# Graph layer and two-of-eight experts: four finer edge groups sorted beside the gathers, expert choices beside the last sums, tiles of 128 tokens, results added into the output

## What is computed

```python
edge_index = jnp.stack([src, dst])
x = x + gnn(_layernorm(x), W1, b1, W2, b2, edge_index)   # agg = segment_sum(x[dst], src); mean = agg / max(cnt, 1)
                                                         # x @ W1.T + b1 + mean @ W2.T + b2
x = x + ffn(_layernorm(x), ...)                          # top 2 of 8 gate scores, softmax over the two
                                                         # y_e = relu(x @ w1[e].T + b1[e]) @ w2[e].T + b2[e]
```

## Time and profile before

| | us |
|---|---|
| median of 3 runs (3217.92 to 3227.65) | 3221.21 |
| span of the profiled execution, first to last instruction | 3186.2 |
| first gather of an edge chunk starts | 376.2 |
| last sum into `agg` starts | 2027.6 |
| expert stage (transposes of its first tile, to its last bias) | 2195 to 3106 |

### The profile page before, as it was taken

How to read it: one execution, slowest core, us unless ns; L and a number is a source line. 1 busy time by engine, 2 the same in 40 slices (tenths; PEclk the granted TensorE clock), 3 DMA queues, 4 the chain that set the end, 5 groups by cost and what they waited for, 6 DMA issues and landing times. The chain is left out here.

```text
span 3186.2 us, 48030 instructions
## 1 busy us (share of the span) xinstructions
PE 2074.3 (65%) x8300; PEld 1438.4 (45%) x8300; DVE 1359.1 (43%) x4519; ACT 1351.9 (42%) x4253; POOL 1193.9 (37%) x1295
## 2 busy tenths in 40 slices
PE   0078766665646655566555555657899888898980
PEld 0056523333323333333333333444777777777770
DVE  7988677555558555555223223464000000000005
ACT  5156634655644555565444444445222222222220
POOL 1011276444447544445666666100222222222220
PEclk9999856778765777777666666556999999999995
DMA  3001122212332222224322224520212221221217
GB/s 101 0 24 35 50 79 80 63 59 63 58 61 79 68 66 64 66 65 72 94 86 89 89 86 86 77 93 14 74 48 89 89 68 52 87 89 46 73 30 244
DMA packets 104790, 227.36 MB, mean 71 GB/s; under 512 B 23170, under 2 KB 63530, under 8 KB 100644
## 3 DMA queue, kind: packets, MB, share of 16 engines
q0 software_dynamic: 55296, 151.07, 18.1%
q1 hardware_dynamic: 49444, 75.77, 7.2%
HBM read 282.12 MB, written 33.93 MB: 99 GB/s over the span
## 5 line engine op out<-in xcount | busy, mean ns | idle before, releaser
L411 POOL DMA_INDIRECT arena<-ytab,stage x928 | 907.2, 978 | 346.5 <-issue 264.1
L694 PE MATMUL bank<-arena,onehot 128*128 128x257 f32 x1856 | 786.8, 535 | 334.2 <-issue 102.6
L694 PEld LDWEIGHTS bank<-arena,onehot 128*128 128x128 f32 x1856 | 425.1, 263 | 590.0 <-issue 352.8
L647 PE MATMUL bank<-ohc,val 125*128 125x336 f16 (+3 forms) x1796 | 412.0, 344 | 402.8 <-ACT val L486 210.1
L977 DVE TENSOR_TENSOR agg<-agg,bank 128x257 f32 x928 | 388.7, 419 | 596.0 <-PE bank L694 235.9
L486 ACT ACTIVATE val<-ohq,arena 125x128 f16<-125x128 f16 (+1 forms) x1370 | 462.9, 391 | 380.2 <-DVE ohq L883 282.6
L591 ACT ACTIVATE arena<-bank,agg 128x256 f32<-128x256 f32 x448 | 212.5, 474 | 683.4 <-PE bank L745 646.9
L647 PEld LDWEIGHTS bank<-ohc,val 125*128 125x128 f16 (+1 forms) x1796 | 155.6, 109 | 645.8 <-ACT val L486 317.6
L529 ACT ACTIVATE onehot<-away 128x128 f32<-128x128 f32 x928 | 277.7, 299 | 397.5 <-PE bank L694 185.7
L757 PE MATMUL bank<-agg,arena 128*128 128x256 f32 x1792 | 400.6, 382 | 0.0
L745 PE MATMUL bank<-xnT,agg 128*128 128x256 f32 x1792 | 398.8, 381 | 0.8 <-DVE xnT L1110 0.8
(11 more groups left out here) (148 smaller groups left out, 1173.1 us busy)
## 6 DMA issues: line engine op xcount, KB each, us to landing
agg<-in_w SPq DMA_DIRECT2D x112, 1024.0 KB
arena<-ytab,stage POOLq DMA_INDIRECT x928
agg<-ztab SPq DMA_DIRECT2D x12, 896.0 KB, 7.3
agg<-in_b SPq DMA_DIRECT2D x56, 128.0 KB
ytab<-yout SPq DMA_DIRECT2D x7, 896.0 KB, 4.1
xtab<-xn SPq DMA_DIRECT2D x49, 128.0 KB, 1.7
node<-in_x SPq DMA_DIRECT2D x4, 1536.0 KB
out<-node SPq DMA_DIRECT2D x6, 896.0 KB
```

The source lines that it names most:

```text
L411: pool.indirect_dma_start(out=rows[:, r, 0:D], out_offset=None, in_=ytab[:, :], in_offset=bass.IndirectOffsetOnAxis(ap=stage[:, r:r + 1], ...
L647: mm = pe.matmul(bank[4 + v][:, 0:n], val[0:lanes, u % RING[g], v, :], ohc[0:lanes, u % RING[g], 0:n], start=False, stop=False, skip_group ...
L694: pe.matmul(bank[r % NPS][:, 0:W], onehot[:, r % NPS, :], rows[:, r, :], start=True, stop=True).then_inc(s_agg, 1)
```

## The change

Most of the file is new; the arithmetic on features is as before, except where noted.

- **Edges.** Four groups (128, 176, 240, 256 columns). The edges of a group are sorted without padding to chunks and cut into *units* of 256 (two gathers): 63, 86, 118 and 125 units, 784 gathers. A *segment* is a unit's share of one source block: 589 run. Each takes two accumulating 257-column matmuls and one sum into `agg`. POOL's indices come straight from `rowidx`.
- **Ranks** come from PE: triangular f16 matmuls (`rank_part`) over one-hot tiles of 16 columns x 50 (`block_onehots`, 125x800 f16), picked out by DVE (`picked_ranks`).
- **Placing** goes by tiles of 8 columns, one DVE instruction for eight one-hots (`place_tile`); ACT scales 8 columns one at a time (4 of 8 in group 0).
- **Lane one-hots** of four segments are one DVE instruction (`lane_onehots`, 128x1024 f16), widened to float32 by one ACT instruction.
- **Order.** Everything about the segments is written out, no loop; `share(window, total, k)` spreads the sort of the next group over the segments k of this one. The W1 half of the linear layer moves from the start to beside the last group (`self_part`). The mean is taken out of the weights and not of x, so that x is transposed as it is.
- **Between the layers.** `tail(r)` does row r of h, moments, transposes, gates, choices and token sort beside the last 51 segments; blocks are done in the order in which the last units reach them. The first 14 blocks' tokens fill 10 early tiles from a table of their own (`xtab_a`), and the rest of the choices are made beside those tiles.
- **Experts.** T = 128, 106 tiles, `fetch` three tiles ahead. The softmax weight of each row is gathered too (`fetch_weights`, 4 bytes a row) and applied by DVE. h goes to `out` before, and `deliver` adds into `out` with an accumulating scatter that waits until the one before has landed. The end stage is gone.

The core of the diff:

```diff
-COLS = [229, 278, 293]
+COLS = [128, 176, 240, 256]
...
+HALVES = 2
+UNIT = HALVES * P
+UNITS = [-(-EP * c // UNIT) for c in COLS]
...
+SEGS = [-(-(u + NT - 1) // 8) * 8 for u in UNITS]
...
+RU = 8
+BACK = 4
+WIDE = 16
...
+PC = 8
...
+QUAD = 4
...
+NA = 10
...
+T = 128
...
-R = 16
...
-T = 256
```

Gathers, POOL. `s_free` counts units whose segments are multiplied:

```diff
-                        pool.indirect_dma_start(out=rows[:, r, 0:D], out_offset=None, in_=ytab[:, :],
-                                                in_offset=bass.IndirectOffsetOnAxis(ap=stage[:, r:r + 1], axis=0)).then_inc(s_row[r], 16)
...
-                    gathers(i, False)
+                pool.wait_ge(s_rowtab, g + 1)
+                for k in range(UNITS[g]):
+                    v = UNIT0[g] + k
+                    if v >= RU:
+                        pool.wait_ge(s_free, v - RU + 1)
+                    for h in range(HALVES):
+                        c = HALVES * k + h
+                        pool.indirect_dma_start(out=rows[:, v % RU, h, 0:D], out_offset=None, in_=ytab[:, :],
+                                                in_offset=bass.IndirectOffsetOnAxis(ap=rowidx[g % 2][:, c:c + 1], axis=0)).then_inc(s_row[v % RU], 16)
```

Segments, PE (new), and DVE:

```diff
+                        upto = [n_units & COUNTS for n_units in loaded(ENG.PE, need[g % 2], k // 2, m // 2, UNIT0[NG])]
+                    if k % QUAD == 0:
+                        pe.wait_ge(s_oh, n // QUAD + 1)
+                    if k % 2 == 0:
+                        pe.wait_ge(s_units, upto[k % 16 // 2])
+                    if n >= NPS:
+                        pe.wait_ge(s_sum, free_after(n))
+                    pair = rows_flat[:, bass.ds(at[k % 16], HALVES * W)]
+                    for h in range(HALVES):
+                        mm = pe.matmul(bank[bank_of(n)][:, 0:W], onehot[n // QUAD % 2][:, n % QUAD, h, :], pair[:, h * W:(h + 1) * W],
+                                       start=(h == 0), stop=(h == HALVES - 1))
+                    mm.then_inc(s_agg, 1)
+                    if k >= LAG:
+                        beside(g, k - LAG)
+                for k in range(RUN[g] - LAG, RUN[g]):
+                    beside(g, k)
...
+                    if k % 16 == 0:
+                        at = loaded(ENG.DVE, offs[g % 2], k, min(16, SEGS[g] - k), (NT - 1) * W)
+                    if k % QUAD == 0 and n // QUAD + 1 < SEG0[NG] // QUAD:
+                        lane_onehots(n // QUAD + 1)
+                    v.wait_ge(s_agg, n + 1)
+                    if n > 0:
+                        v.wait_ge(s_sum, n)
+                    a = agg[:, bass.ds(at[k % 16], W)]
+                    v.tensor_tensor(a, a, bank[bank_of(n)][:, 0:W], ALU.add).then_inc(s_sum, 1)
+                    beside(g, k)
```

Ranks picked, columns placed and lanes, DVE (new):

```diff
+                v.wait_ge(s_ta, k)
+                if t == 0:
+                    v.tensor_copy(c3[s % 2][0:NT, :], rank_a[0:NT, TH:TH + 3]).then_inc(s_c3, 1)
+                v.tensor_tensor(prod[0:EP, 0:TH], rank_a[0:EP, 0:TH], oh[j % OHB][0:EP, 0:TH], ALU.mult).then_inc(s_ma, 1)
+                v.wait_ge(s_tb, k)
+                v.tensor_tensor(prod[0:EP, TH:2 * TH], rank_b[0:EP, 0:TH], oh[j % OHB][0:EP, TH:2 * TH], ALU.mult).then_inc(s_mb, 1)
+                v.wait_ge(s_ma, k)
+                v.wait_ge(s_mb, k)
+                v.tensor_reduce(pos[0:EP, t * WIDE:(t + 1) * WIDE], prod[0:EP, :].rearrange("p (u b) -> p u b", b=BW), AX.X, ALU.add).then_inc(s_v, 1)
+                n_v.up()
...
+            def place_tile(s, i):
+
+                j, c = PT0[s] + i, i * PC
+                if j >= 2:
+                    v.wait_ge(s_pt, j - 1)
+                v.tensor_tensor(in_pairs(ohq[j % 2][0:EP]), counted(PC, P), pairs(pos_cq[0:EP, 1, c:c + PC, :], PC, P), ALU.is_equal).then_inc(s_q, 1)
+                v.tensor_tensor(in_pairs(ohc[j % 2][0:EP, :, 0:CH[s]]), counted(PC, CH[s]), pairs(pos_cq[0:EP, 0, c:c + PC, :], PC, CH[s]),
+                                ALU.is_equal).then_inc(s_c, 1)
+                v.wait_ge(s_q, j + 1)
+                if s == 0:
+                    m = PC - BY_ACT
+                    v.tensor_tensor(in_pairs(val[j % 2][0:EP, BY_ACT:PC, 0, :]), in_pairs(ohq[j % 2][0:EP, BY_ACT:PC]),
+                                    pairs(val1_2[0:EP, c + BY_ACT:c + PC, :], m, P), ALU.mult)
+                c += COL0[s]
+                v.tensor_tensor(in_pairs(val[j % 2][0:EP, :, 1, :]), in_pairs(ohq[j % 2][0:EP]), pairs(val2_2[0:EP, c:c + PC, :], PC, P), ALU.mult).then_inc(s_vd, 1)
...
+                    v.wait_ge(s_oh, q - 1)
+                m = QUAD * HALVES
+                v.tensor_tensor(onehot16[q % 2].rearrange("p k (m r) -> p k m r", r=2),
+                                lanes16[:, :].rearrange("p (a m r) -> p a m r", a=1, r=2).to_broadcast([P, m, P // 2, 2]),
+                                lane2[g % 2][:, k:k + QUAD].rearrange("p k h (a r) -> p (k h) a r", a=1).to_broadcast([P, m, P // 2, 2]),
```

Experts, POOL and DVE:

```diff
-            def deliver(j, b):
+            def fetch_weights(j, b):
+                table = ptab_a if isinstance(j, int) and j < NA else ptab
+                pool.wait_ge(s_pst, j + 1)
+                pool.sem_inc(s_pass)
+                for n in range(TT):
+                    pool.indirect_dma_start(out=weight[:, b, n:n + 1], out_offset=None, in_=table[:, :],
+                                            in_offset=bass.IndirectOffsetOnAxis(ap=pstage[:, b, n:n + 1], axis=0)).then_inc(s_pg[b], 16)
+
+            def deliver(j, b, landed):
                 pool.wait_ge(s_sst, j + 1)
                 pool.wait_ge(s_fo, j + 1)
+                if landed is not None:
+                    pool.wait_ge(s_sc2[1 - b], 16 * TT * landed)
                 pool.sem_inc(s_pass)
                 for n in range(TT):
-                    pool.indirect_dma_start(out=ztab[:, :], out_offset=bass.IndirectOffsetOnAxis(ap=sstage[:, b, n:n + 1], axis=0),
-                                            in_=ysb[:, b, n, :], in_offset=None).then_inc(s_sc2[b], 16)
+                    pool.indirect_dma_start(out=out[:, :], out_offset=bass.IndirectOffsetOnAxis(ap=sstage[:, b, n:n + 1], axis=0),
+                                            in_=ysb[:, b, n, :], in_offset=None, bounds_check=N - 1, oob_is_err=False,
+                                            compute_op=ALU.add).then_inc(s_sc2[b], 16)
...
                     v.wait_ge(s_sc2[b], half * 16 * TT)
-                v.tensor_tensor(ysb[:, b], bank[5 + b][:, :].rearrange("p (n d) -> p n d", d=D),
-                                b2b[:, b:b + 1, :].to_broadcast([P, TT, D]), ALU.add).then_inc(s_fo, 1)
-
+                v.tensor_tensor(ysb[:, b], out_bank(j, b)[:, 0:TT * D].rearrange("p (n d) -> p n d", d=D),
+                                b2b[:, b:b + 1, :].to_broadcast([P, TT, D]), ALU.add).then_inc(s_fb, 1)
+                v.wait_ge(s_fb, j + 1)
+                v.wait_ge(s_pg[b], (half + 1) * 16 * TT)
+                v.tensor_scalar(ysb[:, b, 0], ysb[:, b, 0], weight[:, b, 0:1], None, ALU.mult).then_inc(s_fo, 1)
+
```

1979 lines of the change are left out of this document (1263 added, 716 removed).

## The result

The changed kernel takes 2154.72 us (median of four runs, 2149.78 to 2161.83) beside 3221.44 of the kernel before: a ratio of 0.669, 95% interval 0.667 to 0.671. The forecast was 2100 us, with a range of 1985 to 2350. Its profiled execution took 2149.78 us with a span of 2148.0.

A forecast was written before the change was run, and what follows sets the result against it. No engine is full in the gather stage, where POOL is busiest; PE is 90% busy in the expert stage. Terms 130 + 1100 + 108 + 722 + 6 = 2066 of span, with 35 around it 2101, so 2100 us; range 1985 to 2350.

The forecast's parts named there:

- Gathers and sums, 1100: Gather stage: from 1651 to 1100 us; the larger bounds by group, 170+221+295+350, sum to 1036; lower end 1000.
- the 6%: Gather stage: allowance for hand-overs among PE, ACT and DVE, on top of the 1036 us; 41 us in the first three groups.
- POOL's floor, 784 x 1.25 = 980: Gather stage: 784 gathers at 0.95 us plus 0.30 of issue; by group 158, 215, 295, 313 us.
- the rival of the slowed gathers: Gather stage: DVE instructions with two SBUF inputs lengthen gathers beside them by 0.33 us; +113 us, 2215 in all; chance 13%.
- DVE as the other bound, 170, 221, 252: First three groups: DVE's us for sorting the next group plus this group's segments at 0.65 us each.
- ACT in the last group, 350: Last group: ACT decides for 35 of the last 51 segments, some 2.5 us where POOL needs 1.8; 350 us with the rest.
- Register loads: DVE in the gather stage: a load costs at most 3.3 us per 16 sums, a share of it in 0.65 us a segment.
- f16 pairs at the float32 pace: DVE's two-tensor f16 instructions gain nothing over float32: 1.23 us for 1024 elements, +225 us, 2325 in all; chance 9% or 8% as listed: 8%.
- hand-overs as before: First three groups run at 60% of their busiest engine, 1143 us for 686; +416 us, 2515 in all; chance 9%.
- Between the layers, 0: Between the layers: from 167 to 0 us, with DVE's last small work and second token sort beside the early tiles.
- Late tiles, 96 x 7.4 + 12: Expert stage: 96 late tiles at 7.4 us with hand-overs, 710, plus 12 us over all expert changes; 722 us.
- Around the span, 35: Whole run: the median of the runs stood 35 us above the old kernel's span, and the new kernel gets the same 35.

The follow-up runs named there:

- the experiment with extra work: Changed kernel plus a repeated two-input f16 comparison on DVE behind each of the first 128 lane one-hots, 88 us in all; 2170.66 us.
- the plain scatter: Changed kernel with expert-stage scatters that write instead of adding, run where the kernel before took 2853.12 us; 2026.74 us, gather stage 1103 us.

## Why the prediction held, and where it was off

**Gathers and sums, 1100 forecast.** This term is the mis-sized one, and its steps need to be taken apart. By the records of the gathers the 1223 us are: 824 of busy time, 239 of issue at 0.30, 136 of longer pauses for slots, 24 from the last gather to the last sum. On the chip without late signals the same code gives 829 + 239 + 9 + 26 = 1103, which is the forecast. That it fits so well is in part luck: the floor was 83 us too low, and the 6% stood in for it. By group it took 187, 241, 327 and 348 us there, where the forecast with its 6% had 180, 234, 313 and 371.

- *POOL's floor, 784 x 1.25 = 980.* The gather is 1.05 us, not 0.95, so the floor is 1063. That is the rival of the slowed gathers, and its mechanism took place: in groups 1 and 2, beside sorting, 1.09 us. A fit of each gather's time to what DVE does beside it gives 0.53 us more per us of the two-input product L1358, 0.28 for the comparison L1521, 0.25 for L1350 and nothing for L1349, 0.09 per us of a sum with one input in PSUM and one in SBUF, and nothing for reduces; its single figures are rough, the experiment with extra work gives 15 us for 66 beside gathers, 0.23. I had priced it at +113 and the floor rose by 83. The Trainium skill, SBUF — State Buffer, section Who interferes with whom, has both sentences that I had weighed; for three of the four f16 instructions the trace agrees with the first, contention at two SBUF inputs, in a weak form: a gather beside them is longer by 0.25 to 0.53 us per us. L1349 has two SBUF inputs too and shows nothing.
- *DVE as the other bound, 170, 221, 252.* With half the gathers the three groups took 181, 230 and 280: 7% over these sums, so the 6% for hand-overs was right as a size of the ring. But it was added to the wrong thing. POOL sets the stage, and hand-overs hide behind it.
- *ACT in the last group, 350.* With half the gathers the group took 278, so ACT alone doesn't need 350; with all of them and no late signals it took 348.
- *Register loads.* The step that was read wrongly. I took the waits for "remote", at most 3.3 us for 16 sums, for the price of a register load, and put a share of it into the 0.65 us a segment. That share did little harm, since with 0.65 DVE's groups came out within 7% in sum. But the waits are something else: with no loads at all they stay. They are PE's late done-signals, found on all chips but one. There they cost the stage about 120 us (1219 to 1223 against 1103), for which no term of mine stood: the mis-sized 1100 lacks just this.

The rival of slowed gathers gave 2215 and the stage 1213; that the measured 1223 lies so near is chance: on the chip without late signals the gathers were slowed as well, and the stage took 1103. Of the other rivals, f16 pairs at the float32 pace are out, with 0.686 us for 1024 elements in place of 1.23. So are hand-overs as before, which would have given the first three groups 1143 us; they took 840.

**Start, 130.** 122.0, inside the ends 105 to 165.

**Between the layers, 0.** 8.7 us from the last sum to the first tile's matmul. PE waits there for the first tile's rows:

```profile
1344.24 0.96 POOL L583 DMA_INDIRECT agg<-xtab_a,arena  x1 [23.57 <-ACT arena L811]
...
1352.12 0.66 PE L1184 MATMUL bank<-ident,agg 128*128 128x128 f32 x2 [3.28 <-DMA agg<-xtab_a,arena]
```

The indices for this gather come last of the token sort, just ahead of the last sum, and its rows land 7.7 us after it starts, where the landings recorded for the edge gathers have a median of 2.8. The DMA engines were full at that time (share 1.03, 358 GB/s), mostly with SP's transfers, the expert weights among them. That these held the rows up is likely, but wasn't tested. The forecast of nothing counted DVE's work on the tail and not the way of the first rows.

**Early tiles, 108.** 87.6, that is 8.8 us each. I had added DVE's serial pieces in the first three tiles; PE is busy 85.6 of 87 us, so they are covered.

**Late tiles, 96 x 7.4 + 12.** 7.25 us each, by start, with PE at 100%. The step on the pace of columns (32 x 0.108 + 16 x 0.216 + turn 0.22, which is 7.13 and was given as 7.2) is right: the trace has 3.57 + 3.46 + 0.22. Loading weights doesn't limit it. The 12 us for changes of expert were too much: PE's L1212 waited 0.9 us in all for `in_b`. The scatter that adds stayed hidden: 1.63 us on POOL and a landing mostly 3.4 to 4 us after its start. In 8 of the 96 tiles the recorded landing took over the 6.1 us that I had named as the threshold, the longest 10.1. POOL waited 9 times for one, up to 4.8 us, and the tiles stayed at their pace, with rows fetched three tiles ahead.

**End, 6.** 10.9. Up to the landing of the last scatter, 4.7 us, the term holds. The other 6.2 had no term. GpSimd closes the program with an instruction DRAIN, which the trace's list has from 2138.9 to 2147.8, 6.0 us past that landing; only the engines' last semaphore steps follow. The kernel before has it too, 3.8 us long, but it began 78 us ahead of the end and was covered by the read-back. With the scatter that only writes it took 9.6 us.

**Around the span, 35.** A mistake of method. In every run behind the forecast time and span differ by 1.7 to 1.8 us. The 35 us were the difference between the profiled execution of the kernel before and its other runs; that much lies between chips (3184 and 3221), and it belongs to no kernel's end. Without it the sum is 2066 and the miss 82 us of span: the 35 us hid nearly half of it.

**What is not known.** Why the done-signals are late on some chips, and whether it is the chip or something else of those runs, since only one set of runs had none. The runs exclude register loads, PE's columns, the bytes gathered and what PE reads; halving the gathers removes them, and fewer slots shorten them. Which part of a gather it is wasn't found out, and the changed kernel itself wasn't run on the chip without them. An estimate for it from the plain scatter's run, since the tile is the same: 2027 us, beside 2853 a ratio of 0.71. The kernel before gains more there, 331 to 368 us, and has more late signals by the count, about 440 us: so part of the 0.669 is likely late signals that the change takes away. Having 784 gathers in place of 928 doesn't give that by the number alone, since 440 to 255 is more than 928 to 784. None of this was tested.

## What to carry to other kernels

Before a wait with an unnamed releaser is given a cause, take that cause away in one run: here one kernel with constants in place of register loads showed that the waits had another cause. Halve the work of each engine that could set a stage, one at a time: half the gathers gave 247 us, half the matmuls 22, although PE was the busier engine of the two. And keep the time of the kernel before beside every run: it told of another chip, without which the plain scatter would have seemed to be worth 130 us.

## What the hardware showed that I had not expected

- Done-signals of matmuls that arrive up to 9.1 us after the recorded end in the changed kernel, 11.6 where PE read other data, for DVE, SP and ACT at once, on the chips of all runs but three; 232 to 277 us in all with 784 gathers of any width and eight slots, 17 us with 392. They come in a burst (four increments within 0.28 us). Behind the one shown PE, which had idled, was granted 0.51 of its clock, the lower level of 1.2 GHz.
- The kernel before takes 2853 us on one chip and 3184 to 3228 on the others, while the late tiles of the changed kernel take 7.25 us on all of them: in the changed kernel the chips differ in the gather stage and not in the pace of PE.
- A scatter that adds holds POOL for 1.63 us, one that writes for 1.01. A gather costs the same for rows of 256 bytes as for rows of 1 KB: 1.045 and 1.051 us.
- GpSimd's closing DRAIN lasts until 6.0 us after the last scatter that adds has landed. So it is in all twelve traces here that end with one.
